# An attention and linear-attention pair: three pieces of the ramp moved (one layer's folded biases, a subtraction, one projection)

## The chip, the cores and the metric

One Trainium2 chip, one of its cores. The metric is the device time of one execution in microseconds (us). The profiled execution gives a span, from the first to the last instruction, and a time of its own.

## The reference

The input x has 32 sequences of 256 rows and 256 columns, in float32. Two layers follow one another.

- Layer 0: `xn = layer_norm(x)`; q, k, v are `xn @ w + b`, with 16 heads of 16; `softmax(q k^T) v` per head; then `layer_norm(y) * (1 + scale) + shift`, silu, a product with out_w, and x is added. scale and shift come from `silu(emb) @ emb_w + emb_b`, one row of 512 per sequence.
- Layer 1: the same frame around linear attention. q has a softmax over each head, k a softmax over time; `k^T v` per head gives a 16 x 16 matrix, which multiplies q. Its scale and shift come from its own emb_w.

The weights and biases of each norm are folded into the projections: the products with the norm's bias ("column" and "row" below) are computed once, at the start. So are the silu(emb) products of both layers ("embeddings").

## The kernel before, in words

Each engine has one instruction stream written out by hand; semaphores tie them together, and nothing is reordered by a planner. The first part of the kernel is a loop over 37 turns (`for t in range(TURNS)`, once per engine). In turn t sequence t is prepared, and older sequences are further along.

TensorE (`pe`, L1615 to L1680) does in a turn, in this order: two row-maximum groups (`rowmax(t, 0)`, `rowmax(t, 1)`, line L1357), a scores group (L1338), the four transposes of the normed input of sequence t (`xturn`, L1409), groups again, the projections `qk(t, 0)` (q), `qk(t, 1)` (k) and `vals(t)` (v), each 12 matmuls at L1261, and between them the products with the probabilities (`values`, L1376, from turn 4 on). Groups of row maxima lag the sequence by 13 eighths of a turn, groups of scores by 28: so row maxima begin in turn 1, scores in turn 3 with `scores(t, 4)`.

A projection is split into high and low parts. The transposed input lies in PSUM bank psX. ScalarE copies it (`xturned`, L590), and VectorE subtracts this copy from the bank for the low part (`xlow`, L953). The first product of the turn, `qk(t, 0)`, waits for that subtraction, because it overwrites the same bank.

Each row-maximum group goes to one of three pairs of banks (psM, psT0, psT1). VectorE reduces it (`maxima(t, i)`, L947), and the pair is free for the next group only then. Until the first group of scores, groups alternate between psM and psT1, and psT0 is left to the one-time products. When the eight maxima of a sequence are there, GpSimd splits them (`csplit`, L422), TensorE turns them (`cturn`, L1386), ScalarE copies them out.

The one-time work sits in the first turns. `embeddings(1)` multiplies layer 1's weights, `embeddings(2)` gathers layer 0's result (8 matmuls at L1302 and L1280, half and half), `embeddings(3)` gathers layer 1's (`gather(1)`, 4 matmuls x 2 records at L1302; `column`, 4 x 2 at L1280), `embeddings(4)` is one row product (L1287). ScalarE's `gathered()` (five operations, L735 to L739) reads the results; VectorE adds the row into `rb` (L1151). The first group of scores waits for both, through p_act and p_ve.

The other places around the change: RAMP (L37) names turns 2 and 3, in which VectorE's `xlow` stands between the first and the second reduction (L1157), and TensorE's `qk(t, 1)` stands before `rowmax(t, 5)` (L1651) instead of after `cturn` (L1660). SyncE issues all transfers, and its order does not change.

Of the kernel before, what the change touches and what calls it, by code (L numbers as in the profile page):

```python
# [32 lines left out]
TURNS = B + 5  # L33
ROUNDS = B + 6
EARLY = 2

RAMP = (2, 3)  # L37


def ok(n):  # L40
# [34 lines left out]
def bass_cond_seq_kernel(nc, x, cond, mask_f, mask_i, weights, emb, cols, rows, ident_d, diag_d, fill, out):  # L75
# [4 lines left out]
    with ExitStack() as ctx:  # L80
# [487 lines left out]
        def _(a):  # L568
# [162 lines left out]
                a.activation(es[:, l, :], psT[0][:, 512 * l:512 * l + 512], ACT.Identity).then_inc(p_act, 1)  # L731

            def gathered():
                a.wait_ge(p_pe, 9)
                a.activation(ev[:, :, :, :], psT[0][:, 0:8 * B].rearrange("p (l o b) -> p l o b", l=2, o=4), ACT.Identity)  # L735
                for o in range(2):
                    a.activation(bq[:, 4 + o:5 + o], psT[0][:, 256 + o:257 + o], ACT.Identity,
                                 bias=col[:, 1, 6 + o:7 + o])
                    ins = a.activation(bq[:, 6 + o:7 + o], psT[0][:, 258 + o:259 + o], ACT.Identity,  # L739
                                       bias=col[:, 1, 16 + o:17 + o])  # L740
                ins.then_inc(p_act, 1)

            for t in range(TURNS):
                if ok(t):
                    xturned(t)
                if t == 0:
                    biases(0)
                if t == 2:
                    embedded(1)
                if t == 3:  # L750
                    gathered()
                if t == B + 2:
                    t_(0, 0)
                exps(t, 0)
                if ok(t - 4):
                    yturn(t - 4, 0)
                exps(t, 1)
                exps(t, 2)
                exps(t, 3)
                if t == B + 2:  # L760
                    a.wait_ge(s_sT, 8 * (B - 3))
                    hh_(0, 0)
                if t == B + 3:
                    xn_(0)
                if ok(t):
                    qk(t, 0)
                if t == 1:
                    a.wait_ge(p_pe, 5)
                    a.activation(tc[:, :, :], psY[:, 0:4 * B].rearrange("p (k b) -> p k b", k=4), ACT.Tanh,
                                 scale=0.5).then_inc(p_act, 1)  # L770
                exps(t, 4)
                if t == B + 2:
                    u_(1, 0, r_f0)
                if ok(t - 4):
                    yturn(t - 4, 1)
                if t == B + 2:
                    t_(1, 0)
                if t == B + 3:
                    xT_(0)
                if ok(t - 2):  # L780
                    cturned(t - 2)
                if t == 0:
                    biases(1)
                exps(t, 5)
                if t == B + 1:
                    u_(0, 0, r_f0)
                if ok(t):
                    qk(t, 1)
                exps(t, 6)
                if t == B + 2:  # L790
                    hh_(1, 0)
                exps(t, 7)
                if t == 1:
                    embedded(0)
            freed(a)
            xn_(1)
            xT_(1)
# [49 lines left out]
        def _(v):  # L847
# [299 lines left out]

            for t in range(TURNS):
                if t == 3:
                    v.wait_ge(p_pe, 8)  # L1150
                    v.tensor_tensor(rb[:, 2, :], rb[:, 2, :], psT[0][:, 512:768], ALU.add).then_inc(p_ve, 1)  # L1151
                if t == B + 3:
                    x1_(0)
                    hl_(1)
                    st0_(0)
                maxima(t, 0)
                if t in RAMP:  # L1157
                    xlow(t)
                maxima(t, 1)
                if ok(t) and t not in RAMP:  # L1160
                    xlow(t)
                if t == 0:
                    first_turn()
                maxima(t, 2)
                if t >= 1 and ok(t + 1):
                    stats(t + 1, 0)
                if ok(t - 5):
                    ystats(t - 5, 1)
                if t == 1:
                    swish()  # L1170
                if t == B + 3:
                    x1_(1)
                    st0_(1)
                maxima(t, 3)
                if t >= 4:
                    for_later(t - 4)
                if t == B + 2:
                    v.wait_ge(s_sT, 8 * (B - 3))
                    h_(0, 0)
                    hl_(0)  # L1180
                maxima(t, 4)
                if t >= 1 and ok(t + 1):
                    stats(t + 1, 1)
                if t == B + 2:
                    h_(1, 0)
                maxima(t, 5)
                maxima(t, 6)
                if t == B + 3:
                    xl_(0)
                if ok(t - 4):  # L1190
                    divide(t - 4, 0)
                maxima(t, 7)
                if ok(t - 4):
                    ystats(t - 4, 0)
                if ok(t):
                    vbias(t)
                if ok(t - 4):
                    divide(t - 4, 1)
# [55 lines left out]
        def _(pe):  # L1254
# [335 lines left out]
            def embeddings(step):  # L1590

                if step == 0:
                    pe.wait_ge(s_qf, 3)
                    pe.wait_ge(p_act, 4)
                    pe.wait_ge(p_film, 2)
                    pe.wait_ge(s_ld[2], 16 * LOADS[2])
                    embed(0).then_inc(p_pe, 1)
                elif step == 1:
                    pe.wait_ge(s_vb, 2)
                    embed(1).then_inc(p_pe, 1)  # L1600
                elif step == 2:
                    pe.wait_ge(s_ld[3], 16 * LOADS[3])
                    pe.wait_ge(p_act, 5)
                    pe.wait_ge(p_sum, 1)
                    gather(0)
                    column(psT[0][:, 256:258], 1, 1)
                elif step == 3:
                    pe.wait_ge(p_act, 6)
                    gather(1)
                    column(psT[0][:, 258:260], 1, 2).then_inc(p_pe, 1)  # L1610
                else:
                    pe.wait_ge(p_act, 6)
                    row(psT[0][:, 512:768], 1, 0).then_inc(p_pe, 1)

            for t in range(TURNS):  # L1615
                rowmax(t, 0)
                rowmax(t, 1)
                scores(t, 0)
                if ok(t):
                    xturn(t)  # L1620
                if t == 2:
                    embeddings(1)
                if t == 3:
                    embeddings(3)
                if ok(t - 4):
                    values(t - 4, 0)
                    values(t - 4, 1)
                scores(t, 1)
                rowmax(t, 2)
                if t == B + 2:  # L1630
                    f0_(1)
                scores(t, 2)
                if t == B + 3:
                    o0_(1)
                if t == 0:
                    first_column()
                if ok(t):
                    qk(t, 0)
                if t == 1:
                    conditions()  # L1640
                if t == 2:
                    embeddings(2)
                scores(t, 3)
                rowmax(t, 3)
                if ok(t - 4):
                    values(t - 4, 2)
                rowmax(t, 4)
                scores(t, 4)
                if ok(t - 4):
                    values(t - 4, 3)  # L1650
                if t in RAMP:  # L1651
                    qk(t, 1)
                rowmax(t, 5)
                scores(t, 5)
                rowmax(t, 6)
                if ok(t - 2):
                    cturn(t - 2)
                if t == B + 1:
                    f0_(0)
                if ok(t) and t not in RAMP:  # L1660
                    qk(t, 1)
                if t == 0:
                    second_column()
                if t == B + 2:
                    o0_(0)
                if t == B + 3:
                    tr_(0)
                if ok(t - 4):
                    yturn(t - 4, 0)
                rowmax(t, 7)  # L1670
                scores(t, 6)
                scores(t, 7)
                if ok(t):
                    vals(t)
                if ok(t - 4):
                    yturn(t - 4, 1)
                if t == 1:
                    embeddings(0)
                if t == 2:
                    embeddings(4)  # L1680
# [97 lines left out]
```

## Time and profile before

| | us |
|---|---|
| median of 3 runs | 901.18 |
| lowest and highest | 900.85, 901.26 |
| profiled execution, its time | 901.26 |
| profiled execution, its span | 899.1 |
| TensorE busy | 863.8 (96%) |
| VectorE busy | 762.9 (85%) |
| ScalarE busy | 670.7 (75%) |
| GpSimd busy | 616.2 (69%) |

The time of the profiled execution is 2.2 us more than its span. Busy shares are of the span. PE is TensorE, PEld its weight loads, DVE is VectorE, ACT ScalarE, POOL GpSimd. Turn 2 runs from about 32.5 to 46.0 us on TensorE, turn 3 from 46.05 to 58.86, turn 4 from 58.86.

### The profile page before, as it was taken

To read this page: it belongs to the slowest core of one execution; us is meant where nothing else is said; L and a number is where in the kernel's file an instruction comes from. 1 tells how busy PE (TensorE), PEld (TensorE's weight loads), DVE (VectorE), ACT (ScalarE), POOL (GpSimd) and SP (SyncE) were. 2 spreads that over 40 slices of the span, in tenths; PEclk is the share of its full clock that TensorE was granted. 3 is DMA by queue.
4 is the path that set the end of the run, shared out by engine and by line. 5 is a ranking of instruction groups with operands and counts; after the bars stand their busy time and mean duration, and the time that the engine had idled before them with its cause. 6 is when DMAs were issued, how large, how long until landed. Compare 5 with 4: busy or idle time off the path is not lost.

```text
span 899.1 us, 23736 instructions
## 1 busy us (share of the span) xinstructions
PE 863.8 (96%) x8432; PEld 718.2 (80%) x8432; DVE 762.9 (85%) x1569; ACT 670.7 (75%) x1200; POOL 616.2 (69%) x1096
## 2 busy tenths in 40 slices
PE   5899999999999999999999898999999999999995
PEld 4677777777777777777776567999999999999985
DVE  5789999999999999999998658888888888888874
ACT  2257777777777777777767868888888888888874
POOL 3456575757575666666664357888888888888864
PEclk9999999999999999999999999999999999999999
DMA  8863535353534344443433322222222222222101
GB/s 263 250 197 109 174 114 184 113 180 116 176 121 165 132 158 138 148 150 139 158 125 135 105 70 94 61 86 90 85 84 83 84 83 83 83 83 83 36 31 59
DMA packets 77396, 108.54 MB, mean 121 GB/s; under 512 B 7072, under 2 KB 43392, under 8 KB 77152
## 3 DMA queue, kind: packets, MB, share of 16 engines
q1 hardware_dynamic: 77280, 107.03, 35.4%
q8 instruction: 68, 1.11, 0.5%
q14 instruction: 48, 0.39, 0.1%
HBM read 35.60 MB, written 16.88 MB: 58 GB/s over the span
## 4 chain that ended last, share of the span: by engine, by line
PE 88%; DVE 4%; issue 2%; ACT 2%; POOL 1%; DMA 1%; SPq 0%; DVEq 0%; ACTq 0%; POOLq 0%
PE psX L1261 16%; PE psY L1376 13%; PE psT L1261 9%; PE psM L1261 9%; PE psT L1357 6%; PE psT L1338 5%; PE psY L1261 5%; PE psT L1523 3%; PE psM L1357 3%; PE psT L1272 3%; PE psY L1491 3%; PE psY L1397 3%; PE psM L1272 3%; PE psM L1338 2%; PE psX L1409 2%
## 5 line engine op out<-in xcount | busy, mean ns | idle before, releaser
L947 DVE TENSOR_REDUCE sb_cm<-psT 128x4 f32<-128x1024 f32 x168 | 202.6, 1217 | 12.1 <-PE psT L1357 12.0
L584 ACT ACTIVATE sb_P<-psT 128x1024 f32<-128x1024 f32 x176 | 177.7, 1026 | 30.0 <-PE psT L1338 14.5
L1376 PE MATMUL psY<-sb_P,sb_Vp 128*17 128x256 f32 x2048 | 129.2, 381 | 1.0 <-DVE sb_yr L973 0.9
L947 DVE TENSOR_REDUCE sb_cm<-psM 128x4 f32<-128x1024 f32 x88 | 107.1, 1217 | 7.7 <-PE psM L1357 7.6
L396 POOL TENSOR_SCALAR sb_ve<-sb_mv 128x2 f32<-128x2 f32 x32 | 7.3, 229 | 134.0 <-DVE sb_mv L981 133.9
L1261 PE MATMUL psX<-sb_xT,sb_W0h 128*128 128x256 f32 x488 | 93.6, 294 | 0.0
L584 ACT ACTIVATE sb_P<-psM 128x1024 f32<-128x1024 f32 x80 | 82.0, 1025 | 14.5 <-PE psM L1338 6.7
L1376 PEld LDWEIGHTS psY<-sb_P,sb_Vp 128*17 128x17 f32 x2048 | 50.6, 97 | 46.8 <-issue 6.1
L413 POOL TENSOR_TENSOR sb_qp<-sb_qp 128x512 fp32r<-128x512 f32 x64 | 82.1, 1283 | 5.3
L1357 PE MATMUL psT<-sb_Ks,sb_Qs 64*128 64x256 f32 x672 | 74.7, 305 | 3.0 <-DVE sb_cm L947 1.9
L1338 PE MATMUL psT<-sb_Qs,sb_Ks 64*128 64x256 f32 x704 | 74.5, 295 | 2.0 <-ACT sb_P L584 1.9
L1261 PEld LDWEIGHTS psX<-sb_xT,sb_W0h 128*128 128x128 f32 x488 | 71.5, 192 | 4.6 <-ACT sb_qp L598 0.2
L1357 PEld LDWEIGHTS psT<-sb_Ks,sb_Qs 64*128 64x128 f32 x672 | 50.1, 185 | 27.2 <-issue 12.9
L1338 PEld LDWEIGHTS psT<-sb_Qs,sb_Ks 64*128 64x128 f32 x704 | 52.8, 185 | 17.3 <-DVE sb_cm L947 8.3
L590 ACT ACTIVATE sb_xT<-psX 128x512 fp32r<-128x512 f32 x32 | 19.1, 597 | 62.1 <-PE psX L1409 62.1
L598 ACT ACTIVATE sb_qp<-psX,sb_bq 128x256 f32<-128x256 f32 x122 | 51.1, 472 | 13.3 <-PE psX L1261 10.9
L458 POOL TENSOR_TENSOR sb_rs<-sb_ve,sb_ph 128x2 f32<-128x2 f32 x64 | 56.4, 882 | 5.3
L494 POOL TENSOR_TENSOR sb_v<-sb_v,sb_qm 128x512 f32<-128x512 f32 x32 | 44.7, 1398 | 21.0 <-DVE sb_qm L1087 20.9
L1261 PE MATMUL psX<-sb_xT,sb_W0l 128*128 128x256 f32 x244 | 48.9, 282 | 0.0
L648 ACT ACTIVATE sb_v<-sb_yr,sb_nm,sb_rs 128x256 f32<-128x256 f32 x64 | 35.0, 595 | 14.2 <-POOL sb_nm L462 14.2
L639 ACT ACTIVATE sb_xn<-sb_v,sb_nm,sb_rs 128x256 f32<-128x256 f32 x64 | 35.0, 595 | 13.7 <-POOL sb_nm L462 13.5
L1081 DVE TENSOR_TENSOR sb_v<-psT,sb_rb 128x512 f32<-128x512 f32 x32 | 22.1, 692 | 26.0 <-PE psT L1261 26.0
(180 smaller groups left out, 2581.5 us busy)
## 6 DMA issues: line engine op xcount, KB each, us to landing
sb_Qs<-sb_qp SPq DMA_DIRECT2D x96, 256.0 KB
sb_Ks<-sb_qp SPq DMA_DIRECT2D x96, 256.0 KB
sb_xt<-in_x SPq DMA_DIRECT2D x32, 256.0 KB, 3.0
y_normed<-sb_Yn SPq DMA_DIRECT2D x32, 256.0 KB, 2.0
sb_u<-in_x SPq DMA_DIRECT2D x32, 256.0 KB, 2.9
sb_u<-y_normed SPq DMA_DIRECT2D x32, 256.0 KB, 3.1
out<-sb_w SPq DMA_DIRECT2D x32, 256.0 KB, 2.2
sb_v<-key_mask SPq DMA_DIRECT2D x32, 128.0 KB, 3.5
```

Source lines behind the costliest of these rows:

```text
L413: g.tensor_tensor(qp[w][:, 1, :, :].bitcast(F32R), qp[w][:, 1, :, :], qp[w][:, 0, :, :], ALU.subtract)\
L458: g.tensor_tensor(rs[:, k], ve[:, k], ph[:, :], ALU.pow).then_inc(e_rs[l], 1)
L494: g.tensor_tensor(q4, q4, qm[:, :].rearrange("p (h a) -> p h a", a=1).to_broadcast([128, 2 * H, DH]), ALU.add).then_inc(e_qs, 1)
L584: a.activation(P[G % 4][:, :], pairs[place["S", n, g][0]][:, :], ACT.Exp).then_inc(s_ex, 1)
L598: ins = a.activation(qp[w][:, 1, o, :], home("qk"[w], n)[:, T * o:T * o + T], ACT.Identity, bias=bq[:, 2 * w + o:2 * w + o + 1])
L639: ins = a.activation(xn[:, i, :], x1[n % 7][:, i, :], ACT.Identity, bias=nm[:, i:i + 1], scale=rs[:, i:i + 1])
L947: v.tensor_reduce(cm[n % 2][:, 4 * j:4 * j + 4], scores, AX.X, ALU.max, negate=True).then_inc(s_mx, 1)
L1261: ins = pe.matmul(dst, part(lhs[a], d, o), part(rhs[b], d, r), start=(m == 0), stop=(m == 5))
L1272: ins = pe.transpose(dst[:, a, 128 * b:128 * b + 128], src[b][:, 128 * a:128 * a + 128], ident[:, :])
L1338: ins = pe.matmul(pair[:, c:c + 256], Ks[n % RING][p:p + 64, g, 128 * m:128 * m + 128].bitcast(F32R), Qs[n % RING][p:p + 64, g, :].bitcast ...
L1357: ins = pe.matmul(pair[:, c:c + 256], Qs[n % RING][p:p + 64, j, 128 * k:128 * k + 128].bitcast(F32R), Ks[n % RING][p:p + 64, j, :].bitcast ...
L1376: ins = pe.matmul(psY[32 * j:32 * j + 17, y0:y0 + T], Vp[n % RING][:, m, 4 * gr + j, :], Pj[:, c0:c0 + 256], start=(m == 0), stop=(m == 1))
```

## The change

Four things move, and none is added or taken away. `embeddings(3)` goes from turn 3 (behind `xturn(3)`) into turn 2, behind `cturn(0)` and ahead of `rowmax(2, 7)`, so it now comes before `embeddings(4)`; the counts that are waited for on p_pe are swapped to match, and an ACT wait that is now redundant goes. `gathered()` moves on ScalarE from turn 3 to the end of turn 2. In turns 2 and 3 `xlow` moves behind `maxima(t, 1)`, where it is in all other turns. In turn 3 `qk(3, 1)` moves from ahead of `rowmax(3, 5)` to behind `cturn(1)`, where it is from turn 4 on; in turn 2 it stays.

```diff
-RAMP = (2, 3)
             def gathered():
-                a.wait_ge(p_pe, 9)
+                a.wait_ge(p_pe, 8)
@@ scalar, for t in range(TURNS)
-                if t == 3:
-                    gathered()
                 exps(t, 7)
                 if t == 1:
                     embedded(0)
+                if t == 2:
+                    gathered()
@@ vector
                 if t == 3:
-                    v.wait_ge(p_pe, 8)
+                    v.wait_ge(p_pe, 9)
                     v.tensor_tensor(rb[:, 2, :], rb[:, 2, :], psT[0][:, 512:768], ALU.add).then_inc(p_ve, 1)
                 maxima(t, 0)
-                if t in RAMP:
-                    xlow(t)
                 maxima(t, 1)
-                if ok(t) and t not in RAMP:
+                if ok(t):
                     xlow(t)
@@ tensor, embeddings, last branch
                 else:
-                    pe.wait_ge(p_act, 6)
                     row(psT[0][:, 512:768], 1, 0).then_inc(p_pe, 1)
@@ tensor, for t in range(TURNS)
-                if t == 3:
-                    embeddings(3)
                 scores(t, 4)
-                if t in RAMP:
+                if t == 2:
                     qk(t, 1)
                 rowmax(t, 5)
                 scores(t, 5)
                 rowmax(t, 6)
                 if ok(t - 2):
                     cturn(t - 2)
-                if ok(t) and t not in RAMP:
+                if ok(t) and t != 2:
                     qk(t, 1)
+                if t == 2:
+                    embeddings(3)
```

## Rows read from the trace of the kernel before

**Rows 1.** The page, part 1: busy us (share) xinstructions, of two engines.
```profile
PE 863.8 (96%) x8432; PEld 718.2 (80%) x8432; DVE 762.9 (85%) x1569; ACT 670.7 (75%) x1200; POOL 616.2 (69%) x1096
```

**Rows 2.** Busy time in one stretch: length; PE, PEld, DVE, ACT, POOL; clock, DMA.
```profile
57.23:72.40 15.17, 15.17 (x178) 11.50 (x177) 12.55 (x19) 11.39 (x17) 8.32 (x16) 1.00 0.38 133
```

**Rows 3.** Chain of waits, 30 to 80 us: start, us, what.
```profile
49.49 1.62 PE psX L1261 x12
...
56.80 0.50 PE psT L1338 x4
57.30 1.63 PE psX L1261 x12
```

**Rows 4.** Timeline, VectorE, turn 2: start, us, instruction, x of them, [idle before <-releaser].
```profile
33.03 1.23 DVE L947 TENSOR_REDUCE sb_cm<-psM 128x4 f32<-128x1024 f32 x1 [0.74 <-PE psM L1357]
34.47 0.69 DVE L953 TENSOR_TENSOR sb_xT<-psX,sb_xT 128x512 fp32r<-128x512 f32 x1 [0.22 <-ACT sb_xT L590]
35.08 1.22 DVE L947 TENSOR_REDUCE sb_cm<-psT 128x4 f32<-128x1024 f32 x1
...
39.06 1.23 DVE L947 TENSOR_REDUCE sb_cm<-psT 128x4 f32<-128x1024 f32 x1 [1.08 <-PE psT L1357]
```

**Rows 5.** Timeline, TensorE, turn 2.
```profile
35.22 0.50 PE L1261 MATMUL psX<-sb_xT,sb_W0h 128*128 128x256 f32 x2
...
42.12 0.30 PE L1386 MATMUL psY<-sb_ident,sb_cx 128*64 128x128 f32 x1
43.13 0.50 PE L1357 MATMUL psT<-sb_Ks,sb_Qs 64*128 64x256 f32 x4 [0.72 <-DVE sb_cm L947]
```

**Rows 6.** Timeline, TensorE, turn 3.
```profile
46.05 0.50 PE L1357 MATMUL psM<-sb_Ks,sb_Qs 64*128 64x256 f32 x4
...
47.22 0.98 PE L1302 MATMUL psT<-sb_sum,sb_es 128*128 128x32 f32 x8
...
48.99 0.50 PE L1357 MATMUL psM<-sb_Ks,sb_Qs 64*128 64x256 f32 x4
49.42 0.50 PE L1261 MATMUL psX<-sb_xT,sb_W0h 128*128 128x256 f32 x2
...
53.70 0.51 PE L1357 MATMUL psT<-sb_Ks,sb_Qs 64*128 64x256 f32 x4
...
54.66 0.30 PE L1386 MATMUL psY<-sb_ident,sb_cx 128*64 128x128 f32 x1
55.66 0.50 PE L1357 MATMUL psT<-sb_Ks,sb_Qs 64*128 64x256 f32 x4 [0.70 <-DVE sb_cm L947]
```

**Rows 7.** Timeline, VectorE, turn 3.
```profile
46.60 1.23 DVE L947 TENSOR_REDUCE sb_cm<-psM 128x4 f32<-128x1024 f32 x1
48.05 0.69 DVE L953 TENSOR_TENSOR sb_xT<-psX,sb_xT 128x512 fp32r<-128x512 f32 x1 [0.22 <-ACT sb_xT L590]
...
51.58 1.23 DVE L947 TENSOR_REDUCE sb_cm<-psT 128x4 f32<-128x1024 f32 x1
52.73 1.22 DVE L947 TENSOR_REDUCE sb_cm<-psM 128x4 f32<-128x1024 f32 x1
...
54.41 3.47 DVE L947 TENSOR_REDUCE sb_cm<-psT 128x4 f32<-128x1024 f32 x3
```

**Rows 8.** Timeline, TensorE and ScalarE, turn 4: turn of the maxima, then qk.
```profile
68.97 0.30 PE L1386 MATMUL psY<-sb_ident,sb_cx 128*64 128x128 f32 x1
69.02 0.48 PE L1261 MATMUL psX<-sb_xT,sb_W0h 128*128 128x256 f32 x2
...
70.73 0.84 ACT L598 ACTIVATE sb_qp<-psX,sb_bq 128x256 f32<-128x256 f32 x2 [0.25 <-PE psX L1261]
```

**Rows 9.** Timeline, ScalarE, turn 3: the copy of the turned input.
```profile
47.41 0.60 ACT L590 ACTIVATE sb_xT<-psX 128x512 fp32r<-128x512 f32 x1 [3.97 <-PE psX L1409]
```

**Rows 10.** Timeline, TensorE: first product of turn 0, and one after an idle stretch.
```profile
11.95 0.80 PE L1261 MATMUL psT<-sb_xT,sb_W0h 128*128 128x256 f32 x2 [0.30 <-DVE sb_xT L953]
...
23.41 0.51 PE L1261 MATMUL psT<-sb_xT,sb_W0h 128*128 128x256 f32 x2 [1.41 <-DVE sb_xT L953]
```

## The prediction

> **What bounds the kernel now.** I read four views. The page's first part says which engine is full: TensorE at 96% [rows 1]. Busy time by stretch says from when: the turn from 57.23 to 72.40 us has 15.17 us of matmul in 15.17 us [rows 2], so from turn 4 on TensorE has no hole, and whatever delays it before 57.23 delays the end. The chain of waits says what it waited for earlier: q of turn 3 (49.49), then maxima on VectorE, then the last scores group of the turn (56.80) and v of turn 3 (57.30) [rows 3]. The timelines give distances. All edits lie before 57.23 in that chain, so the question is one number: when does `vals(3)` start, 57.23 before (0.43 us behind the group at 56.80 [rows 3], the distance that 48.99 to 49.42 shows too [rows 6])?
>
> No work is added. What changes is where holes fall. I walk the chain once.
>
> **xlow in turn 2.** VectorE reduces at 33.03, subtracts at 34.47 and reduces again at 35.08 [rows 4]. A reduction lasts 1.22 but the next starts 1.13 after it: three take 3.47, and (3.47 - 1.22) / 2 = 1.13 [rows 7]. With both reductions ahead, xlow starts at 33.03 + 2 x 1.13 = 35.29, so 0.82 later. q of turn 2 started 0.75 behind xlow (34.47 to 35.22) [rows 4, 5], so it goes to 36.04. Is there slack behind it? No: the fourth reduction, at 39.06, had VectorE idle for 1.08 us waiting for a TensorE group that stands behind q [rows 4]. It goes to 39.88, and all that follows by **+0.82**. The other reading would be that nothing is lost, as the reduction itself comes 0.92 earlier; but that reduction has nobody waiting. So between 0 and 0.82 I take 0.82.
>
> **embeddings(3) in turn 2.** Its length is 48.99 - 47.22 = 1.77 us [rows 6]. Its new place is the hole between cturn(0), 42.12, and rowmax(2, 7), 43.13, in which TensorE waited for a reduction [rows 5]. Behind cturn the next product can start 0.05 later (68.97, 69.02) [rows 8]. So the hole is 43.13 - 42.17 = 0.96 us, and 1.77 - 0.96 = 0.81 sticks out. In times: cturn at 42.94, embeddings from 42.99 to 44.76, rowmax(2, 7) at 44.76: **+1.63** in all against 43.13. Bounds: 0.81 if the hole is used in full, 1.77 if not at all; nothing in it waits (ScalarE copies its input ahead of q's copy of the same turn), so I take 0.81. Behind it stand rowmax(2, 7), v, the row product and turn 3; VectorE's last reduction, its v bias and the addition into rb wait with them.
>
> **Turn 3, up to q.** From rowmax(2, 7) to rowmax(3, 0) it was 46.05 - 43.13 = 2.92 [rows 5, 6]; that order is unchanged, so rowmax(3, 0) is at 47.68 and its reduction 0.55 later (46.05 to 46.60) [rows 6, 7], at 48.23. Here the embeddings are gone from TensorE, 1.77 us less. If nothing else held q, it would start at 49.42 + 1.63 - 1.77 = 49.28. But xlow now has two reductions ahead: 48.23 + 2.26 = 50.49, and q is 0.75 behind that, at **51.24, +1.82** against 49.42 [rows 6]. ScalarE's copy is not late: 1.36 behind rowmax(3, 0) (47.41) [rows 6, 9], so at 49.04. So the 1.77 us taken out of turn 3 become a hole of that size: before, they covered the xlow wait (48.05 + 0.75 = 48.80, while the group at 48.99 still stood ahead of q) [rows 6, 7]. This is the step that decides.
>
> **gathered() on ScalarE.** ScalarE was idle for 3.97 us before the copy at 47.41 [rows 9], so five small operations at about 44.9 fit. They cost nothing, and so does taking them from turn 3: no product waits for ScalarE there. If that cover were gone, scores(3, 4), which waits for them, would be late by their length, at most five times the copy's 0.60, 3.0 us. The wait that `embeddings(4)` loses had been met by then, since `embeddings(3)` waits for the same.
>
> **Turn 3 from q to v.** The reduction that starts behind q was at 51.58 = 49.42 + 2.16, so now 53.40. From there to v the reductions set the pace, unchanged: 57.23 - 51.58 = 5.65, which gives 59.05. The moved k projection must be checked against it. Before, it lay between q and rowmax(3, 5) and cost only time that the reductions covered. Now it follows cturn(1), which is 1.93 behind the reduction at 52.73 (54.66) [rows 6, 7]: that reduction is at 54.55, cturn at 56.48, k at 56.53. It fills the hole of 0.70 that rowmax(3, 7) had [rows 6]. v waits for ScalarE to have emptied the bank: 1.71 + 0.84 behind the start of k (69.02, 70.73) [rows 8], so 59.08, and about 0.06 for the signal (xlow ended at 35.16, q began at 35.22): **59.14, +1.91**. This beats the 59.05 of the reductions by 0.09. Bounds of this move: 0 (the reductions hide it) and 1.62, a projection's length [rows 3], if it were exposed in full.
>
> rowmax(3, 5), at 53.70, also needs the transfers of sequence 2, which had landed by then [rows 6]. They start behind csplit(0), which moves by 0.82, so by 54.52 at the latest; its pair of banks is free only when the reduction of 53.40 ends, at 54.62. Hidden.
>
> **Sum.** 0.82 + 0.81 + 0.19 (q of turn 3) + 0.09 (k) = 1.91 us. The profiled execution took 901.26 (span 899.1 and 2.2 around it): 903.17. It is 0.08 above the median of 901.18, so in medians **903.1 us**, +0.21%.
>
> **Rivals.**
> *Part of it is regained* (0.22). TensorE is idle for 4% of the span [rows 1], some of it behind the loop. If a wait there ends with something not moved, a part is given back; or the hole at 43.13 takes more of the embeddings. Giving back half, 902.1. Against: every wait there hangs on results of the loop itself.
>
> *More is lost* (0.15). rowmax(3, 5) now waits for a reduction as well, and scores(3, 5) for the next; if the k projection then comes out in full beyond the holes, 1.62 - 0.70 = 0.9 us more, 904.0. It decides as soon as TensorE, not VectorE, is last at v. For: three groups and v stand behind k. Against: the sum above, where they end by 58.8.
>
> *The clock* (0.03). The first product took 0.80 for two matmuls, and one behind 1.41 us of idle 0.51 [rows 10]: a short hole has not slowed TensorE, though turn 0 was slow. The new turn has holes of about 0.6 and 1.2 us close together. If it fell there, 12 matmuls of q would take some 0.80 / 0.51 x 1.62 = 2.5, so +0.9: 904.0. The Trainium skill (TensorE: Matmul & The Clock Gate, "What's actually happening") says that activity releases a throttle and idleness brings 1.2 GHz back. The trace agrees for the start by the durations; the granted clock reads 1.00, the 2.4 GHz level, also in rows 2.
>
> *Faster* (0.06). The holes get filled: 0.96 at 43.13 and 0.70 before rowmax(3, 7). If TensorE's own work set the pace in both turns and not VectorE's reductions, 1.66 us of idle would go and only the 0.82 of the first xlow come back: -0.84, 900.3. It decides from the point where xlow(3) starts by 48.5, so that q can follow at 49.28. Against it: two reductions from 48.23 take 2.26 by themselves.
>
> *The forecast* (0.54), own range 902.7 to 903.5.
>
> **How the numbers follow.** What a measurement of this kernel can tell from no change is about 0.2%, 1.8 us, so the border is 902.98, and my forecast is only 0.1 above it. Three quarters of the forecast's weight lie above (0.41), with more lost and the clock (0.18): slower 0.59. The rest of the forecast and nearly all of the part regained: same 0.35. Faster 0.06. The range: the forecast's, down into the part regained and up to the case where k comes out: 901.8 to 904.1. What it leaves out is the faster case, a regain of nearly everything, and a loss beyond the whole k projection.
>
> **What would show it.** In the new trace: xlow of turn 2 at about 35.3, right behind a reduction and with no idle before it; the embeddings' 16 matmul records from 43.0 to 44.8, TensorE without a hole there, rowmax(2, 7) at 44.8; in turn 3 xlow at 50.5 and before q at 51.2 a hole of over a microsecond on TensorE, released by VectorE's sb_xT; v of turn 3 at 59.1, and then turns of 15.17. If q of turn 3 starts before 50, the step on xlow is wrong, and with it the sum. If turns 4 to 30 have another period than 15.17, something other than a one-time shift happened, as each 0.01 there is worth 0.3 us.

## The result and the profile after

| | kernel before | kernel after |
|---|---|---|
| median of 5 runs, us | 901.18 | 905.08 |
| lowest and highest | 900.85, 901.62 | 904.18, 909.79 |
| profiled execution, time and span | 901.26, 899.1 | 906.84, 904.7 |
| mean granted clock of that execution | 1.000 | 0.994 |

The ratio is 1.0054, with a 95% interval of 1.0029 to 1.0080. The forecast was 903.1 us, at most 904.1. The direction was right. The size was not: +3.9 us against +1.9.

The page of the kernel after, its busy shares (against [rows 1]) and the clock over 40 slices of the span, in tenths:

```profile
PE 868.7 (96%) x8432; PEld 722.9 (80%) x8432; DVE 762.5 (84%) x1569; ACT 670.8 (74%) x1200; POOL 616.4 (68%) x1096
...
PEclk9979999999999999999999999999999999999999
```

TensorE is busy for 4.9 us more with the same 8432 matmuls. So they ran slower somewhere, and the third slice of the clock says where. Busy time of the kernel after in stretches (length; PE, PEld, DVE, ACT, POOL; then the granted clock, DMA share, GB/s):

```profile
41.60:45.00 3.40, 3.24 (x28) 2.89 (x29) 3.00 (x5) 1.71 (x8) 2.90 (x8) 1.00 0.06 18
45.00:48.40 3.40, 3.40 (x15) 3.03 (x14) 1.64 (x2) 0.27 (x2) 3.23 (x6) 0.50 0.24 90
48.40:51.80 3.40, 2.10 (x18) 1.25 (x16) 3.00 (x4) 0.60 (x1) 1.24 (x1) 0.99 0.61 221
51.80:55.20 3.40, 2.97 (x14) 2.75 (x14) 2.02 (x4) 0.00 (x1) 0.00 (x0) 0.51 0.96 260
55.20:58.70 3.50, 2.02 (x24) 1.59 (x24) 2.96 (x5) 1.86 (x3) 0.47 (x3) 0.99 0.55 141
58.70:62.10 3.40, 3.40 (x19) 3.04 (x17) 2.16 (x2) 1.43 (x3) 3.03 (x8) 0.50 0.03 9
```

Three stretches stand at 0.50, the 1.2 GHz level, with stretches at the 2.4 GHz level between them. Ahead of the second and the third, TensorE had waited (2.10 us busy of 3.40 in the third row, 2.02 of 3.50 in the fifth). Ahead of the first it had run `embeddings(3)` and was busy for 3.24 of 3.40 us. TensorE's timeline of the kernel after, against [rows 5, 6] (its L1257 is L1261 before, L1353 is L1357):

```profile
31.80 0.50 PE L1353 MATMUL psM<-sb_Ks,sb_Qs 64*128 64x256 f32 x4
...
35.35 0.51 PE L1257 MATMUL psX<-sb_xT,sb_W0h 128*128 128x256 f32 x2 [0.80 <-DVE sb_xT L951]
...
42.40 0.98 PE L1298 MATMUL psT<-sb_sum,sb_es 128*128 128x32 f32 x8
43.21 1.03 PE L1276 MATMUL psT<-sb_col,sb_W 128*128 128x1 f32 x8
44.17 0.50 PE L1353 MATMUL psT<-sb_Ks,sb_Qs 64*128 64x256 f32 x4
...
46.17 1.05 PE L1257 MATMUL psX<-sb_W0h,sb_xT 128*128 128x256 f32 x4
47.02 1.73 PE L1283 MATMUL psT<-sb_W,sb_col 128*128 128x256 f32 x4
48.68 0.50 PE L1353 MATMUL psM<-sb_Ks,sb_Qs 64*128 64x256 f32 x4
...
52.23 0.80 PE L1257 MATMUL psX<-sb_xT,sb_W0h 128*128 128x256 f32 x2 [1.23 <-DVE sb_xT L951]
...
62.82 0.50 PE L1257 MATMUL psX<-sb_W0l,sb_xT 128*128 128x256 f32 x2
```

Read it by distances from the first group of turn 2, since the two executions differ ahead of any edit: it is at 31.80 here and at 32.48 before. (In one a VectorE operation at 18.58 took 1.23 us, in the other the same one took 0.88.) Four matmuls of a product take 1.05 us at 46.17, and took 0.64 before; the row product takes 1.73 instead of 1.02. VectorE's two subtractions, against [rows 4, 7], stand right behind a reduction, with no idle before them, as forecast:

```profile
34.61 0.68 DVE L951 TENSOR_TENSOR sb_xT<-psX,sb_xT 128x512 fp32r<-128x512 f32 x1
...
51.49 0.68 DVE L951 TENSOR_TENSOR sb_xT<-psX,sb_xT 128x512 fp32r<-128x512 f32 x1
```

And from v of turn 3 on the turn is as long as before [rows 2]:

```profile
62.82:78.00 15.18, 15.18 (x178) 11.51 (x177) 12.78 (x19) 11.72 (x17) 6.90 (x14) 1.00 0.37 130
```

So it is a one-time shift, made between 32 and 63 us.

### The profile page after: what moved, and what is told of

It is laid out like the page before. It is cut to its first block, busy times and chain, and to the rows that moved or that the text cites. A ratio compares the mean times of both kernels' runs of the same rounds, so it can differ in the third digit from the quotient of the medians.

```text
span 904.7 us, 23736 instructions
## 1 busy us (share of the span) xinstructions
PE 868.7 (96%) x8432; PEld 722.9 (80%) x8432; DVE 762.5 (84%) x1569; ACT 670.8 (74%) x1200; POOL 616.4 (68%) x1096
## 4 chain that ended last, share of the span: by engine, by line
PE 88%; DVE 3%; issue 3%; ACT 2%; POOL 1%; DMA 1%; SPq 0%; DVEq 0%; ACTq 0%; POOLq 0%
PE psX L1257 16%; PE psY L1372 13%; PE psT L1257 9%; PE psM L1257 9%; PE psT L1353 6%; PE psT L1334 5%; PE psY L1257 5%; PE psT L1519 3%; PE psT L1268 3%; PE psM L1353 3%; PE psY L1487 3%; PE psY L1393 3%; PE psM L1268 3%; PE psM L1334 2%; PE psX L1405 2%
## 5 line engine op out<-in xcount | busy, mean ns | idle before, releaser
L1257 PE MATMUL psX<-sb_xT,sb_W0h 128*128 128x256 f32 x488 | 95.5, 298 | 2.0 <-DVE sb_xT L951 2.0
L1257 PEld LDWEIGHTS psX<-sb_xT,sb_W0h 128*128 128x128 f32 x488 | 73.2, 196 | 6.5 <-DVE sb_xT L951 2.4
L1353 PE MATMUL psT<-sb_Ks,sb_Qs 64*128 64x256 f32 x672 | 74.9, 306 | 2.0 <-DVE sb_cm L945 1.4
L1353 PEld LDWEIGHTS psT<-sb_Ks,sb_Qs 64*128 64x128 f32 x672 | 50.3, 186 | 26.3 <-issue 13.9
L1257 PE MATMUL psX<-sb_xT,sb_W0l 128*128 128x256 f32 x244 | 49.8, 286 | 0.0
L620 ACT ACTIVATE sb_v<-psM,sb_FB,sb_FA 128x256 f32<-128x256 f32 x64 | 32.7, 561 | 15.4 <-PE psM L1268 15.4
```

What stands on the lines that cost most here:

```text
L1257: ins = pe.matmul(dst, part(lhs[a], d, o), part(rhs[b], d, r), start=(m == 0), stop=(m == 5))
L1353: ins = pe.matmul(pair[:, c:c + 256], Qs[n % RING][p:p + 64, j, 128 * k:128 * k + 128].bitcast(F32R), Ks[n % RING][p:p + 64, j, :].bitcast ...
```

## The experiments

One reading aid for all: mean clock. A stretch of some 3.4 us at half clock takes 1.7 / 904 = 0.0019 off the mean over the span. So an execution at 1.000 had none, one at 0.998 had as much as one of them, at 0.994 three. The mean is over the whole span. Of the 14 profiles of this case, five (e3, e4, e5, e8, e12) have slow time in the last 10 us, which no edit touches, and e3, e8 and e12 have it nowhere else. So a mean clock counts slow stretches but doesn't say where they lie; only a profile does. Each kernel was executed 10 to 12 times beside 35 executions of the kernel before on its chip. "At clock 1.000" is the mean of the executions that had that clock, and "by order" means what the order of the work costs with the clock at 1.000.

Three theories stood. A: order costs what was forecast, and the slow clock, set off by where the embeddings stand, costs the rest. B: the same, but set off by the holes from xlow. C: order makes it all, the clock is a bystander.

### One part undone, or the holes filled

**e1: embeddings(3) and gathered() back in turn 3.**

```diff
+                if t == 3:
+                    gathered()          # scalar; counts of p_pe swapped back
+                if t == 3:
+                    embeddings(3)       # tensor, behind xturn
```

> The kernel after, with embeddings(3) and gathered() back in turn 3; xlow and the k projection stay moved. In the kernel after the granted clock stood at about 0.5 in three stretches (45.0 to 48.5, 51.9 to 55.2, 58.7 to 61.9 us), and these hold some 4.2 us of the 6.3 us lost from turn 2 to v of turn 3. Theory A (the clock, set off by where embeddings(3) stands: matmuls of 32 and 1 columns next to a wait): by order alone 0.82 for xlow in turn 2, 0.19 for q, 0.09 for k, 1.1 us in all; the clock stays at 1.00, time about 902.3. Theory B (the clock, set off by the holes that xlow leaves in turns 2 and 3, wherever the embeddings stand): a slow stretch remains near 50 us or later, clock 0.996 to 0.998, time 903.5 to 904.5. Theory C (order alone makes the loss, the clock is a bystander): about 903.5, between the two kernels, at any clock.

Measured: median 903.43, ratio 1.0015 (1.0001 to 1.0030), mean clock 0.9955, two executions at clock 1.000: 901.04 and 901.43. The profiled one was slow at an unexpected place, in turn 1:

```profile
17.90:21.30 3.40, 0.62 (x5) 0.47 (x5) 3.17 (x6) 0.50 (x2) 1.93 (x2) 1.00 0.91 328
21.30:24.70 3.40, 2.65 (x15) 2.25 (x13) 0.77 (x2) 0.60 (x1) 0.69 (x2) 0.55 0.98 287
24.70:28.10 3.40, 2.73 (x12) 2.63 (x12) 1.39 (x4) 0.00 (x0) 0.25 (x1) 0.50 1.03 280
```

TensorE had been busy for 0.62 us of 3.40 ahead of it, in a part of the ramp that is the same in both kernels. It was idle for 2.78 us in one piece, waiting for this operation of VectorE:

```profile
18.48 2.30 DVE L882 SCALAR_TENSOR_TENSOR sb_W0l<-sb_W,sb_col,sb_W0h 128x256 fp32r<-128x256 f32 x2
```

This pair of operations took 0.88 or 1.23 us in all other profiles but that of e10, where it took 2.31, the idle time was 2.78 again, and the clock was slow from 22.0 to 28.8 us. So a place for the slow clock can come from one execution and not from the order. Neither A nor B is right about the place: the ramp has many spots where the clock can fall. The order part came out smaller than expected, about 0.7 (901.24, the mean of two, against 900.55 for the kernel before beside it) against 1.1.

**e2: xlow between the first two reductions again.**

```diff
                 maxima(t, 0)
+                if t in (2, 3):
+                    xlow(t)
                 maxima(t, 1)
-                if ok(t):
+                if ok(t) and t not in (2, 3):
```

> The kernel after, with xlow between the first two reductions again in turns 2 and 3; embeddings(3) stays in turn 2, the k projection of turn 3 stays moved. By order alone: embeddings 0.9 us at the last row maxima of turn 2, of which 0.3 are left at q of turn 3 since xlow is early there, and 0.1 for k: 901.5. Theory A (place of the embeddings sets the clock off): the clock still falls near 45 us and v of turn 2 runs slow, about 1.6 us more, clock 0.996 to 0.998, time about 903. Theory B (holes from xlow): clock 1.00, time 901.5. Theory C (order alone): 901.5 to 902, whatever the clock.

Measured: median 903.59, ratio 1.0023 (1.0007 to 1.0039), mean clock 0.9947, at clock 1.000 901.24 (two). The profiled execution was slow from 44.1 to 47.7, behind the moved embeddings, as in the kernel after, and TensorE had been busy for all of the 3.40 us ahead of it:

```profile
40.70:44.10 3.40, 3.40 (x32) 3.05 (x33) 3.08 (x6) 1.67 (x7) 2.85 (x8) 1.00 0.18 57
44.10:47.70 3.60, 3.60 (x16) 3.02 (x14) 1.68 (x2) 0.32 (x3) 3.43 (x6) 0.53 0.27 103
```

The place isn't enough, though: in the profiles of e3 and e5 the same matmuls stand there and the clock stays at 1.00 behind them. A half hit: the order cost 0.7 (expected 0.4), and there are about as many slow stretches as in the kernel after, with xlow early.

**e3: the k projection back ahead of rowmax(3, 5).**

```diff
-                if t == 2:
+                if t in (2, 3):
                     qk(t, 1)
```

> The kernel after, with the k projection of turn 3 back ahead of rowmax(3, 5). Theory A and B: the first two slow stretches stay as they are (v of turn 2, q of turn 3); the third had fallen on the k projection behind cturn(1), where it could not be hidden; here the projection lies beside reductions. Order gives 0.1 back, the third slow stretch up to 1.2: time 903.8 to 905, clock 0.993 to 0.997. Theory C: 905, no difference beyond 0.1.

Measured: median 904.52, ratio 1.0025 (1.0011 to 1.0038), mean clock 0.9950, one execution at 1.000: 902.17. In the expected span. By that one execution the third move is worth 0.2 us by order. The distance from q to v of turn 3 in the profile, clean in the ramp, is the better measure: 7.82 us, and 7.81 in the kernel before, against 7.91 with the move (e7 below), so 0.1. Whether the move also adds a slow stretch is within the scatter.

**e4: 14 idle products in the holes of turn 3.**

```diff
+                if t == 3:
+                    filler(4, (p_act, 7))    # 128x248 products into psT0
                 rowmax(t, 2)
+                if t == 3:
+                    filler(10)
```

> The kernel after, with 14 idle products of 248 columns added on TensorE in the holes of turn 3: 4 ahead of rowmax(3, 2), 10 between it and q. They write a part of psT0 that nobody reads. They fit in the holes of 0.5 and 1.2 us, so by order alone they cost nothing, at most 0.3 us. Theories A and B: the slow stretch on q of turn 3 (51.9 to 55.2) does not come, nor perhaps the one after it; the first, at 45.0 to 48.5, comes as before. Time 902.4 to 903.8, clock 0.996 to 0.999. Theory C: the time of the kernel after, 905, or more.

Measured: median 905.48, ratio 1.0031 (1.0019 to 1.0043), mean clock 0.9960, two at clock 1.000: 902.22 and 902.27. A miss in the median. The clock was slow from 40.5 to 43.9, from 57.3 to 60.8 and at the end instead, and not at 51.9. That the filling kept it from falling there is not shown: e5's profile has no slow stretch at 51.9 either, without any filling.

What these four showed without being asked: the kernel before has slow stretches too. Of its 35 executions beside them 7 were at 1.000 (900.1 to 901.0 us) and the rest reached up to 905.5.

### Both kernels on one chip, and all holes filled

**e5: the kernel after. e6: the kernel before.** No edit.

> The kernel after, unchanged, in many executions beside the kernel before on one chip. In the first series the executions with granted clock 1.000 took 900.1 to 901.0 us for the kernel before and 902.4 for the kernel after; each slow stretch of 3.4 us at half clock lowers the mean clock by 0.0019. Theory A (order 1.9, and more slow stretches after than before): among executions at clock 1.000 the two kernels differ by 1.6 to 2.0 us; by medians they differ by 3 or more, and the mean clock is lower after (0.994) than before (0.996). Theory C (order alone): the two differ by as much at clock 1.000 as by medians, and their clocks are alike.

> The kernel before, unchanged, for a profile of an execution of its own and more executions: its profile had a clock of 1.000 throughout, while 28 of its 35 executions of the first series had not. Expected: 900.5 us where the clock is 1.000, and a slow stretch of 3.4 us somewhere between 20 and 60 us or after 860 in the profile, with products of 12 matmuls at 2.9 instead of 1.6 us in it. Theory C would have the clock low in it without the time changing.

Measured: e5 median 904.45, ratio 1.0037 (1.0019 to 1.0056), mean clock 0.9946 against 0.9964. None of its 12 executions was at 1.000, so the comparison asked for rests on the one execution of the kernel after in the first series, 902.43, and on a straight line through time and clock of all: 902.37 us at 1.000 for the kernel after (41 executions, these 12 and the 29 recorded with the result), 900.63 for the kernel before (115; the 25 at 1.000 average 900.48). The profile of e5 is clean until 56 us, and that makes it the best test of the forecast's steps:

```profile
31.70 0.50 PE L1353 MATMUL psM<-sb_Ks,sb_Qs 64*128 64x256 f32 x4
...
44.08 0.50 PE L1353 MATMUL psT<-sb_Ks,sb_Qs 64*128 64x256 f32 x4
...
46.99 0.50 PE L1353 MATMUL psM<-sb_Ks,sb_Qs 64*128 64x256 f32 x4
...
50.54 0.50 PE L1257 MATMUL psX<-sb_xT,sb_W0h 128*128 128x256 f32 x2 [1.23 <-DVE sb_xT L951]
...
55.84 0.48 PE L1257 MATMUL psX<-sb_xT,sb_W0h 128*128 128x256 f32 x2
...
59.83 0.51 PE L1257 MATMUL psX<-sb_W0l,sb_xT 128*128 128x256 f32 x2
```

e6 had median 902.18, ratio 1.0004 (0.9988 to 1.0020), and its profiled execution, of the kernel before, was slow 1.2 us behind `embeddings(2)`:

```profile
35.80:39.20 3.40, 3.08 (x31) 2.86 (x29) 2.28 (x5) 0.81 (x2) 0.00 (x0) 1.00 1.01 293
39.20:42.70 3.50, 3.42 (x18) 3.20 (x20) 2.36 (x4) 0.02 (x1) 1.40 (x4) 0.52 0.69 183
```

In it v of turn 3 is late by 1.46 us: it starts 26.21 us behind the first group of turn 2 (58.31 and 32.10), against 24.75. Up to 0.47 of that is a wait of the k product for ScalarE just ahead of the slow stretch; the rest is the clock. Of the expectations, e6's held. e5's is untested at clock 1.000 on this chip, its mean clock is as expected, and its medians differ by 2.9 (expected 3 or more). Theory C fell: within one kernel, time follows the clock.

**e7: fillers in turns 2 and 3 and inside both embeddings.** The edit of e4, and:

```diff
+                if t == 2:
+                    filler(6, (p_act, 5))    # ahead of qk(2, 0)
                     gather(0)
+                    filler(4)
                     gather(1)
+                    filler(4)
```

> The kernel after with 28 idle products of 248 columns on TensorE (they write a part of psT0 that nobody reads): 6 in the hole ahead of q of turn 2, 4 between the two halves of embeddings(2) and 4 between those of embeddings(3), 4 and 10 in the holes of turn 3. The 8 in the embeddings are not hidden and cost 8 x 0.12, about 0.9 us by order. If holes and narrow matmuls set the clock off, there is no slow stretch between 33 and 56 us in the profile, the mean clock rises from 0.994 to 0.997 or more (stretches before 33 us, near 57 and at the end stay), and the median is 903.5 to 904.5, with the executions at 1.000 near 903.2. If the clock falls for another reason, the clock stays at 0.994 and the median rises to 906.

Measured: median 905.03, ratio 1.0029 (1.0013 to 1.0046), mean clock 0.9959. Its profile has no slow stretch at all, and gives the order with the moves made and the fillers in:

```profile
51.12 0.51 PE L1257 MATMUL psX<-sb_xT,sb_W0h 128*128 128x256 f32 x2
...
59.03 0.50 PE L1257 MATMUL psX<-sb_W0l,sb_xT 128*128 128x256 f32 x2
```

The fillers put rowmax(2, 7) off by 0.91 us against e5, near the 0.9 expected. But the two executions at 1.000 took 902.00 and 902.29, no longer than the kernel after and not 903.2, so their cost does not show in the whole time. The mean clock went from 0.9946 to 0.9959, within the scatter of 12 executions, and the median did not fall. Inconclusive.

### What sets the clock off: narrow against wide

**e11 and e12: the kernel before with extra work of one length and two widths.**

```diff
 # e11, in embeddings(2) and likewise in embeddings(3)
                     column(psT[0][:, 256:258], 1, 1)
+                    column(psT[0][:, 256:258], 1, 1)
 # e12
                     gather(0)
+                    filler(8)
```

> The kernel before with the column products of embeddings(2) and embeddings(3) done twice: 4 more matmuls of one column in each, about 0.96 us each, same result. By order up to 1.9 us, 0.96 of it sure (the first one is on the way to the reductions; of the second a part lies beside xlow). Theory D (what sets the clock off is not only waiting but narrow matmuls, in which TensorE counts as busy): more slow stretches than in the kernel before, mean clock 0.994 or less against 0.9964, so median 904 to 905.5. Without D: clock 0.996, median 903 to 903.5.

> The counterpart of the run with doubled columns: 8 idle products of 248 columns in each of the two places (8 x 0.12 = 0.95 us each), so the same delay, but wide. Theory D: the mean clock is 0.997 or more, fewer slow stretches than in the kernel before in spite of the longer ramp; at clock 1.000 it takes 902 to 902.5, median 902.5 to 903.3, clearly under the narrow one. Without D: the two runs agree in clock and time.

Measured: narrow, median 903.60, ratio 1.0022 (1.0011 to 1.0033), mean clock 0.9945, no execution of 12 at 1.000. Wide, median 902.41, ratio 1.0005 (0.9994 to 1.0016), mean clock 0.9977. In slow stretches, wherever they lie: 2.9 per execution against 1.2, and 1.6 for the kernel before beside them. The forecasts of size missed by a little: the narrow median and clock were to be 904 or more and 0.994 or less, the wide median 902.5 or more. The comparison is Theory D's all the same: same delay, and a lower clock with the narrow work. Drawing 12 and 12 of the 24 executions at random gives a difference of mean clock as large as 0.0032 in about one case of a thousand. Wide work did not raise the clock above that of the kernel before by more than the scatter. The profile of e11 shows it in two rows, and what TensorE did in the first of them:

```profile
47.60:51.00 3.40, 3.40 (x31) 3.25 (x31) 2.62 (x4) 1.29 (x6) 1.69 (x2) 1.00 0.61 221
51.00:54.40 3.40, 3.40 (x22) 2.95 (x21) 2.23 (x5) 1.16 (x3) 0.00 (x0) 0.51 0.94 277
```

```profile
47.10 0.98 PE L1302 MATMUL psT<-sb_sum,sb_es 128*128 128x32 f32 x8
47.91 1.93 PE L1280 MATMUL psT<-sb_col,sb_W 128*128 128x1 f32 x16
```

TensorE was busy for 3.40 us of 3.40 (and of the 3.40 before those), and the clock fell all the same. In e12's profile the ramp is clean, and the one slow stretch lies at the end, from 894 us on.

### An order that beats both

**e8: the column half of embeddings(2) into the hole.**

```diff
                     gather(0)
-                    column(psT[0][:, 256:258], 1, 1)
                 if ok(t - 2):
                     cturn(t - 2)
+                if t == 2:
+                    column(psT[0][:, 256:258], 1, 1)
```

> The kernel before, with one edit meant to gain: the second half of embeddings(2) (the column product, 0.96 us) goes from ahead of rowmax(2, 3), where VectorE waited 1.08 us for TensorE, into the hole of 0.96 us behind cturn(0). By order rowmax(2, 3), its reduction, and all that hangs on the reductions come 0.93 us earlier, and the hole is filled: 899.6 at clock 1.000 against 900.5. Theory A: no new hole arises, so the slow stretches are as many as before or fewer: median 0.9 to 1.3 us under the kernel before. Rival: the column product next to cturn makes the narrow stretch in which the clock falls, as embeddings(3) did there, and eats the gain: median as before or 0.5 above.

Measured: median 901.19, ratio 0.9992 (0.9978 to 1.0006); five at clock 1.000, mean 900.37, against 900.29 for the seven of the kernel before beside it and 899.6 expected. Order gained nothing. ScalarE's q copy of turn 2 and the k product behind it say why:

```profile
38.05 0.84 ACT L598 ACTIVATE sb_qp<-psX,sb_bq 128x256 f32<-128x256 f32 x2 [3.32 <-DMA sb_Qs<-sb_qp]
```

```profile
38.94 0.50 PE L1261 MATMUL psX<-sb_xT,sb_W0h 128*128 128x256 f32 x2 [1.28 <-ACT sb_qp L598]
```

The rival I had written down (a new narrow stretch) did not come: clock 0.9971. A third thing did, a transfer. The copy writes sb_qp, and waits for the transfer that still reads it. It started at 37.87 us in the kernel before and starts at 38.05 here, though the first group of turn 2 comes 0.74 us earlier (31.74 against 32.48). The slow time of this profile lies at the end of the span:

```profile
891.20:894.60 3.40, 2.44 (x12) 2.18 (x12) 0.69 (x1) 0.00 (x0) 2.40 (x2) 0.50 0.30 103
894.60:898.00 3.40, 1.21 (x6) 0.91 (x5) 0.69 (x1) 0.00 (x0) 0.00 (x0) 0.50 0.16 54
```

These two stretches together cost 0.9 us (901.30 against 900.37), about 0.5 each.

**e9: e8, and the two output weight loads issued in turn 5. e10: the late loads alone.** (Left out here: the new semaphore, VectorE's wait for it, and the count of the old one, from 5 to 3.)

```diff
-                for l in range(2):
-                    sp.dma_start(Wo[l][:, :, :], weights[:, l, 3]).then_inc(s_ld[3], 16)
+                if t == 5:
+                    for l in range(2):
+                        sp.dma_start(Wo[l][:, :, :], weights[:, l, 3]).then_inc(s_wl, 16)
```

> The kernel before with two edits. The column half of embeddings(2) goes behind cturn(0), as in the run before; and the two loads of the output weights (512 KB) leave SyncE's queue ahead of the parts of sequence 1 and are issued in turn 5, with a semaphore of their own. Before, the order gain of 0.93 us did not come: ScalarE's q copy of turn 2 waited for the q parts of sequence 1 until 38.05 us, and TensorE's k product with it (idle 1.28). If that landing was the new bound, it comes some 1.5 us earlier (512 KB at about 350 GB/s) and executions at clock 1.000 take 899.4 to 899.8 (kernel before 900.3 to 900.6), median about 1 us under the kernel before. If the landing is set by something else, it is no different from the run before: 900.4 at clock 1.000.

> The kernel before with the late loads alone. In its order the copy that waits for the parts had 0.5 us of slack to the k product when turn 2 begins at 32.5, and none when it begins at 31.7: 0 to 0.4 us gain, 900.0 to 900.5 at clock 1.000. If the gain is as large as with both edits, the column product is worth nothing.

Measured: e9 median 900.00, ratio 0.9983 (0.9970 to 0.9997); six at clock 1.000, mean 899.41, where the kernel before beside it had 900.58 (ten); mean clock 0.9980, the highest of all, though not clear of the scatter. e10 median 902.46, ratio 1.0000 (0.9987 to 1.0013), at clock 1.000 900.55. So each half alone is worth nothing and together they give 1.2 us at clock 1.000. In e9 the copy starts as soon as its product ends, and the k product does not wait:

```profile
37.15 0.84 ACT L600 ACTIVATE sb_qp<-psX,sb_bq 128x256 f32<-128x256 f32 x2 [1.48 <-PE psX L1264]
```

```profile
38.52 0.50 PE L1264 MATMUL psX<-sb_xT,sb_W0h 128*128 128x256 f32 x2
```

e9 beats both kernels, with an interval that ends just below 1.

## Why the prediction was wrong, step by step

Delays against [rows 5, 6], counted from the first group of turn 2 (32.48 before, 31.70 in e5, 31.80 in the profile of the result):

| start of | forecast | e5, clock 1.00 to 56 us | profile of the result |
|---|---|---|---|
| q of turn 2 | +0.82 | +0.82 | +0.81 |
| rowmax(2, 7) | +1.63 | +1.73 | +1.72 |
| rowmax(3, 0) | +1.63 | +1.72 | +3.31 |
| q of turn 3 | +1.82 | +1.90 | +3.49 |
| v of turn 3 | +1.91 | +3.38 | +6.27 |

- **xlow in turn 2** was right, to 0.01. **xlow in turn 3** too: the hole ahead of q is 1.23 us, released by VectorE's subtraction, and q is delayed by 0.18 beyond what came with it (forecast 0.19).
- **embeddings(3) in turn 2** cost 0.91 instead of 0.81. Behind cturn it started 0.14 later (42.26, 42.40), not 0.05.
- **k of turn 3** started 24.14 us behind the first group in e5 (55.84), forecast 24.05. The clock fell in the middle of it. The profile of e7 is clean there: from q to v of turn 3 it is 7.91 us, forecast 7.90 (59.14 - 51.24), and 7.81 before. So this move cost 0.10, forecast 0.09.
- **The sum of the order part** was right: forecast 1.91; 1.90 at q in e5 and 0.10 from there, 2.0 in all; 1.7 to 1.9 between the two kernels at clock 1.000 (902.37 to 902.43, and 900.48 to 900.63). That of the kernel after rests on one execution and a line.
- **The step that failed is the rival named "the clock"**, with chance 0.03 and a price of 0.9 us. Its sentence "a short hole has not slowed TensorE" rested on one row with 1.41 us of idle in one execution. In the profile of the result the clock cost 1.59 us from rowmax(2, 7) to rowmax(3, 0), 1.24 more on q of turn 3 (2.86 us from its start to the next group, 1.62 before), and what is left of 6.27 - 1.91 = 4.4 on the way to v, k most of all. I had looked at holes only. `embeddings(3)`, whose 16 records have 32 and 1 columns, was moved, and I had counted narrow matmuls as work like any other. That its new place added slow stretches is argued from e2's rows and from e11 and e12, not shown: e1, which undid it, has a mean clock within the scatter of the kernel after. The price itself was near: q of turn 3 cost 1.24 more, where 0.9 was written. What failed is the chance, and that one fall was counted where three came.
- Over all executions the kernel after averages 905.91 us and the kernel before 902.04. Of these 3.9 us, 1.7 to 1.9 are order. The rest, about 2.0, is the clock: it costs the kernel before 1.4 to 1.6 us (902.04 against 900.63 by the line, 900.48 at 1.000) and the kernel after 3.5 (905.91 against 902.37).
- The count went up: 1.8 slow stretches per execution before, 2.9 after. By the slopes of the lines each costs 0.8 us before and 1.2 after, but the profiles hardly show a difference in the ramp. On the way to v of turn 3 one cost 1.0 to 1.5 in the kernel before (e6), 1.4 in the kernel after (e5, 3.38 - 2.0), and 1.4 each in the profile of the result ((6.27 - 2.0) / 3). At the end of the span one cost about 0.5 (e8). So a likely reason for the slopes, not shown, is that more of the slow time of the kernel before lies at the end; the executions without a profile don't say where theirs lies.
- The forecast also took the kernel before as free of this, since its profile was. Only 25 of its 115 later executions were, so the base of the sum was a lucky one. Its five executions in the result lie within 0.8 us, and its 115 in the later series within 6.4. A part of the 3.9 us of the medians may be that luck; on one chip the ratio was 1.0037, not 1.0054, though the intervals overlap.

What stays open: which of the three moves adds how many slow stretches. e1, e2 and e3 had 2.4, 2.8 and 2.6 per execution against 2.9, a scatter that 12 executions do not resolve. Whether narrow work or the waits did more in the kernel after is open too.

## What to carry to other kernels

A profile is one execution. Before you price an edit that makes or moves waits in a ramp, look at the granted clock of several executions, and price a hole twice: its own length, and the products behind it at half rate (about 1.4 us for each slow stretch in the kernel after). When you move small work, look at what it stands next to. Extra one-column matmuls lowered the clock here although TensorE was busy, and wide work of the same length did not. Keeping narrow matmuls apart from each other and from waits is worth trying, but no run here has tested it by itself. And when a computed gain does not come, look for a transfer that sits at a fixed time: two edits that each gave nothing gave 1.2 us together.

## What the runs showed of the hardware that was not expected

- TensorE's granted clock fell to half for about 3.4 us, or about twice that (e1, 21.7 to 28.5 us), at changing places of the ramp, from 21 to 63 us, and in the last 10 us of the span. In one unchanged program the place differed: the kernel after at 45.0, 51.9 and 58.7 us in one profile, at 56.3 and 892.6 in another. In 115 executions of the kernel before the mean clock lay between 0.990 and 1.000 and the time between 899.6 and 906.0.
- It fell behind idle stretches (0.62 us busy of 3.40, e1) and behind narrow work without any idle (3.40 of 3.40, e11 and e2). The Trainium skill (TensorE: Matmul & The Clock Gate, "A second HAM failure mode: psum-queue depth-cycling") says that short idles between groups of matmuls can make the clock swing between its two levels. The rows of the kernel after agree for two of its three slow stretches (2.10 us busy of 3.40 and 2.02 of 3.50 ahead of them, with waits of 0.50 to 1.23 us); ahead of the first it was busy for 3.24. e11's rows go beyond it, since there was no idle.
- In turn 0 of every profile products ran at the slow rate (0.80 us for two, [rows 10]) while the granted clock read 1.00, so ahead of the first recorded change durations are the better witness.
- A pair of VectorE operations of one size (sb_W0l, 128x256 each, in turn 1) took 0.88 us in eight profiles, 1.23 in four and 2.30 or 2.31 in two, and TensorE's wait for it grew with it, to 2.78 us.
